# A grouped convolution with a mixture of experts behind it: aggregation on 32 by 64 tiles ahead of the first convolution, weights at the head of both load queues

## What is computed

```
x = x + conv(x, L0_weight, 9 taps, 4 groups) + (cond @ c_weight.T)[:, :, None] + fside[None, :, None]
h   = gelu(gelu(cond @ W0 + b0) @ W1 + b1)
att = softmax(h @ W2 + b2)                       # 128 samples by 8 experts
x = x + einsum('boi,bih->boh', einsum('bk,koi->boi', att, weight), x) + (att @ bias_k)[:, :, None]
```

## Time and profile before

| | us |
|---|---|
| median of 3 runs | 252.88 (252.79 to 253.17) |
| the profiled execution | 252.83 |
| its span in the profile | 251.0 |

### The profile page before, as it was taken

The page is one execution under the profiler, slowest core; times in us unless marked ns, Lnnn a source line. Parts: engine busy times, 40 slices in busy tenths (PEclk is TensorE's granted clock), DMA queues, the critical chain, the costliest instruction groups (busy, mean ns, idle before and its releaser), DMA issues.

```text
span 251.0 us, 5804 instructions
## 1 busy us (share of the span) xinstructions
PE 239.5 (95%) x2180; PEld 95.4 (38%) x2180; DVE 223.1 (89%) x146; ACT 89.5 (36%) x144; POOL 27.1 (11%) x52
## 2 busy tenths in 40 slices
PE   7399999999999999999999999999999999999973
PEld 5263233333333333333333344344444444434531
DVE  0531899999999999999999999999999999999683
ACT  2305353321433333341505233333415052333453
POOL 1030422010101010010101010100101010101000
PEclk9659999999999999999999999999999999999999
DMA  6999693999999999999999999998989998444376
GB/s 145 262 306 274 136 200 60 334 231 407 329 375 240 381 240 339 293 319 305 272 350 238 387 228 373 276 361 249 335 292 287 342 262 347 167 167 168 123 293 256
DMA packets 29770, 68.72 MB, mean 274 GB/s; under 512 B 3312, under 2 KB 5616, under 8 KB 29760
## 3 DMA queue, kind: packets, MB, share of 16 engines
q1 hardware_dynamic: 19824, 51.41, 63.0%
q10 hardware_dynamic: 9936, 17.17, 26.2%
HBM read 35.02 MB, written 33.55 MB: 273 GB/s over the span
## 4 chain that ended last, share of the span: by engine, by line
PE 93%; DMA 2%; DVE 2%; SPq 1%; issue 0%; ACT 0%; DVEq 0%
PE yps L534 64%; PE zps L557 21%; DMA xin<-in_x 2%; PE yps L616 2%; PE yps L573 2%; PE zps L516 2%; DVE xph L414 1%; SPq L199 1%; DVE ynat L483 1%; PE zps L596 0%; PE yps L596 0%; PE zps L585 0%; PE zps L634 0%; DVE ycol L476 0%; ACT xin L380 0%
## 5 line engine op out<-in xcount | busy, mean ns | idle before, releaser
L534 PE MATMUL yps<-xph,wraw 64*64 64x512 f32 x1488 | 167.4, 591 | 0.0
L308 ACT ACTIVATE zout<-zps,gamu 128x512 f32<-128x512 f32 x120 | 72.9, 688 | 130.9 <-PE zps L557 87.9
L534 PEld LDWEIGHTS yps<-xph,wraw 64*64 64x64 f32 x1488 | 60.0, 132 | 100.2 <-issue 99.8
L422 DVE STREAM_TRANSPOSE ycol<-yps 128x1024 f32<-128x1024 f32 x62 | 74.5, 1220 | 9.2 <-PE yps L534 8.5
L414 DVE STREAM_TRANSPOSE xph<-xin 128x2112 f32<-128x2112 f32 x32 | 74.8, 2339 | 2.5 <-DMA xin<-in_x 2.5
L432 DVE STREAM_TRANSPOSE ynat<-ycol 128x2048 f32<-128x2048 f32 x30 | 67.6, 2291 | 1.1
L557 PE MATMUL zps<-ynat,mixv 64*64 64x512 f32 x480 | 57.6, 589 | 0.0
L244 POOL COPY mixv<-mixt 128x512 f32 (+1 forms) x16 | 17.5, 1094 | 178.9 <-ACT zout L308 174.5
L557 PEld LDWEIGHTS zps<-ynat,mixv 64*64 64x64 f32 x480 | 19.9, 132 | 30.3 <-issue 29.3
L316 ACT ACTIVATE mixt<-zps 128x1024 f32<-128x1024 f32 x8 | 7.8, 1021 | 17.3 <-PE zps L516 17.3
L616 PE MATMUL yps<-zout 128*128 128x256 f32 x20 | 8.9, 632 | 2.2 <-POOL zout L250 1.3
(11 more groups left out here) (54 smaller groups left out, 29.1 us busy)
## 6 DMA issues: line engine op xcount, KB each, us to landing
out<-zout SPq DMA_DIRECT2D x60, 512.0 KB, 5.3
xin<-in_x ACTq DMA_DIRECT2D x60, 258.0 KB, 7.5
xin<-in_x SPq DMA_DIRECT2D x60, 258.0 KB, 7.3
out<-xin SPq DMA_DIRECT2D x2, 512.0 KB, 3.2
out<-xin SPq DMA_DIRECT2D x4, 256.0 KB, 2.2
xin<-in_x ACTq DMA_DIRECT2D x4, 132.0 KB, 5.0
xin<-in_x SPq DMA_DIRECT2D x4, 130.0 KB, 5.0
xin<-in_x SPq DMA_DIRECT2D x4, 128.0 KB, 6.7
```

What stands on the lines that cost most here:

```text
L308: nc.scalar.activation(zout[:, o].rearrange("p (i c j q) -> p c i j q", i=2, c=2, q=PH)[:, c], zps[:, at:at + BANK].rearrange("p (q i j) - ...
L422: nc.vector.transpose(ycol[:, :, :, :, :, g].rearrange("p i s j q c -> p (i s j) q c"), yps[:, 2 * BANK * (g % 2):2 * BANK * (g % 2) + 2 * ...
L534: last = nc.tensor.matmul(yps[C * c:C * c + C, at:at + BANK].rearrange("p (s f) -> p s f", s=S // 2), wsum[rows, b, g], xph[slot][c][rows, ...
```

## The change

- The expert weights are stored once (64 columns, 128 KB instead of 256 KB). `aggregate` has two steps instead of four; each step has 8 matmuls on tiles of 32 by 64, four row tiles by two column tiles, where one column tile gives one half of the output channels and the other the other half. `mixt` now holds each matrix once.
- Both steps stand ahead of the first convolution group, with `keep_on(3)` before the attention's matmul, before the first step and before the second; `keep_on(6)` is gone. The output constants come after the first block of group 1, the pair constants after group 3.
- ScalarE instead of VectorE spreads the attention, in four instructions. ScalarE instead of GpSimd fills `mixv`, in four instructions per unit (each 64 partitions by 256 elements, from either half of `mixt` to either half of `mixv`), behind evacuation 1 and the loads of the unit before.
- SyncE's queue starts with `mlps`, `shares`, `mixw`, then all of x of unit 0; ScalarE's starts with `wraw`. ScalarE's loads of unit 1 are issued in two blocks, around the spreading of the attention; its load of unit 2 comes right after the gathers.
- VectorE's first two phase transposes follow each other, and both of unit 1 come one place earlier.

```diff
-        mixt = sb("mixt", [P, C, NS])
+        mixt = sb("mixt", [P, CH // 2, RT * RO, NS])
...
-        mixw = zout[:, 1, 0:CH * P].rearrange("p (a c) -> p a c", a=CH)
-        consts = zout[0:CK, 1, CH * P:]
+        mixw = zout[:, 1, 0:CH * C].rearrange("p (a c) -> p a c", a=CH)
+        consts = zout[0:CK, 1, 2 * CH * C:]
...
+        def mix_places(slot, h, d):
+            return mixv[slot][C * h:C * h + C].rearrange("p b (a d c) -> p d b a c", a=CH // 2, d=2)[:, d]
+        def mix_values(u, d):
+            return mixt[C * d:C * d + C, :, :, bass.ds(S * u, S)].rearrange("p a c b -> p b a c")
...
             sp.dma_start(mlps[:], mlp).then_inc(mlp_in, 16)
-            for k in range(KQ):
-                for t in range(2):
-                    sp.dma_start(*x_piece(0, 0, 0, k, t, 0)).then_inc(x_first, 16)
             sp.dma_start(shares[:], share).then_inc(share_in, 16)
-            for k in range(KQ):
-                for t in range(2):
-                    sp.dma_start(*x_piece(0, 0, 0, k, t, 1)).then_inc(x_in[0], 16)
-            sp.dma_start(wraw[:], conv_w).then_inc(w_in, 16)
+            sp.dma_start(mixw, mix_w).then_inc(mix_in, 16)
+            for part, there in ((0, x_first), (1, x_in[0])):
+                for k in range(KQ):
+                    for t in range(2):
+                        sp.dma_start(*x_piece(0, 0, 0, k, t, part)).then_inc(there, 16)
...
-                nc.gpsimd.tensor_copy(mixv[slot][:], mixt[:, :, bass.ds(S * u, S)].rearrange("p c b -> p b c")
-                                      ).then_inc(mixv_made, 1)
...
+            def matrices(u, slot):
+                for h in range(2):
+                    for d in range(2):
+                        nc.scalar.activation(mix_places(slot, h, d), mix_values(u, d), ACT.Copy).then_inc(mixv_made, 1)
...
+            act.dma_start(wraw[:], conv_w).then_inc(w_in, 16)
             for k in range(KQ):
                 for t in range(2):
                     act.dma_start(*x_piece(0, 0, 1, k, t, 0)).then_inc(x_first, 16)
...
-            act.dma_start(mixw, mix_w).then_inc(mix_in, 16)
...
-            load(1, 1)
+            load_block(1, 1, 0)
+            act.wait_ge(share_in, 16)
+            act.wait_ge(mm, 4)
+            for o in range(RO):
+                nc.scalar.activation(attt[:, o], sps[:, 0:NS], ACT.Copy, scale=turn[:, o:o + 1]).then_inc(soft, 1)
+            load_block(1, 1, 1)
             gather(0, 0)
             gather(0, 1)
             gather(1, 0)
             gather(1, 1)
+            load(2, 0)
...
                         evacuate(2 * i + c - 4, c, o)
                         if o == 1:
                             load(2 * i + c, c)
+                            matrices(2 * i + c - 3, 1 - c)
...
-            dve.wait_ge(mm, 4)
-            nc.vector.tensor_tensor(attt, sps[:, 0:NS].unsqueeze(1).broadcast_to([P, RO, NS]),
-                                    turn.unsqueeze(2).broadcast_to([P, RO, NS]), ALU.mult).then_inc(soft, 1)
             phases(0, 0, 1)
             y_columns(0, 0)
+            phases(1, 1, 0)
             y_columns(0, 1)
-            phases(1, 1, 0)
+            phases(1, 1, 1)
             y_columns(0, 2)
-            phases(1, 1, 1)
             y_columns(0, 3)
...
-                    nc.tensor.matmul(zps[:, BANK * r:BANK * r + BANK], mixw[32 * r:32 * r + 32, a],
-                                     attt[32 * r:32 * r + 32].rearrange("p o b -> p (o b)"),
-                                     start=True, stop=True).then_inc(agg_mm, 1)
+                    for d in range(2):
+                        nc.tensor.matmul(zps[C * d:C * d + C, BANK * r:BANK * r + BANK],
+                                         mixw[32 * r:32 * r + 32, 2 * a + d],
+                                         attt[32 * r:32 * r + 32].rearrange("p o b -> p (o b)"),
+                                         start=True, stop=True).then_inc(agg_mm, 1)
...
+            keep_on(3)
             pe.wait_ge(share_in, 16)
             pe.wait_ge(soft, 3)
             nc.tensor.matmul(sps[:, 0:NS], att[:].rearrange("p o e -> p (o e)"), eye,
                              start=True, stop=True).then_inc(mm, 1)
-            pe.wait_ge(turned, 1)
-            keep_on(6)
+            keep_on(3)
+            first_aggregate()
+            keep_on(3)
+            second_aggregate()
             pe.wait_ge(w_in, 16)
-            conv(0, 0, 0, (first_aggregate,))
-            conv(0, 0, 1, (second_aggregate,))
-            conv(0, 0, 2, (output_constants, None, third_aggregate))
-            conv(0, 0, 3, (None, None, fourth_aggregate))
-            conv(1, 1, 0, (None, None, pair_constants))
+            pe.wait_ge(w_sum, 1)
+            conv(0, 0, 0)
+            conv(0, 0, 1, (output_constants,))
+            conv(0, 0, 2)
+            conv(0, 0, 3, (None, None, pair_constants))
+            conv(1, 1, 0)
             conv(1, 1, 1)
             mix(0, 0, 0)
```

More of the change, by code:

```diff
@@ L237, in _, with constants_of @@
         def _(pool):
-            def matrices(u, slot):
+            def constants_of(u, slot):
                 if not (isinstance(u, int) and u < 2):
                     pool.wait_ge(z_made, 8 * u - 8)
-                if isinstance(u, int) and u == 0:
-                    pool.wait_ge(agg_out, 2 * CH)
-                nc.gpsimd.tensor_copy(mixv[slot][:], mixt[:, :, bass.ds(S * u, S)].rearrange("p c b -> p b c")
-                                      ).then_inc(mixv_made, 1)
                 if isinstance(u, int) and u == 0:
@@ L259, in _ @@
             for a in range(CH):
-                own = mixw[:, a].rearrange("p (d h g c) -> p d h g c", d=2, h=2, g=G)[:, :, :, a]
-                nc.gpsimd.tensor_tensor(own, own, same.rearrange("p (h c) -> p h c", h=2).unsqueeze(1)
-                                        .broadcast_to([P, 2, 2, 8]), ALU.add).then_inc(mix_eye, 1)
+                own = mixw[:, a].rearrange("p (h g c) -> p h g c", h=2, g=G)[:, :, a]
+                nc.gpsimd.tensor_tensor(own, own, same.rearrange("p (h c) -> p h c", h=2), ALU.add).then_inc(mix_eye, 1)
             pool.wait_ge(w_in, 16)
@@ L282, in _, with load_block @@
                                         ALU.mult, ALU.mult).then_inc(const_sum, 1)
-            matrices(0, 0)
-            matrices(1, 1)
+            constants_of(0, 0)
+            constants_of(1, 1)
             with pool.Fori(1, NU // 2) as i:
                 for c in range(2):
-                    matrices(2 * i + c, c)
+                    constants_of(2 * i + c, c)
         @block.scalar
         def _(act):
+            def load_block(u, slot, k):
+                for t in range(2):
+                    act.dma_start(*x_piece(slot, u, 1, k, t)).then_inc(x_in[slot], 16)
             def load(u, slot):
-                if not (isinstance(u, int) and u < 2):
-                    act.wait_ge(turned, 2 * u - 2)
+                act.wait_ge(turned, 2 * u - 2)
                 for k in range(KQ):
-                    for t in range(2):
-                        act.dma_start(*x_piece(slot, u, 1, k, t)).then_inc(x_in[slot], 16)
+                    load_block(u, slot, k)
             def evacuate(u, slot, o):
@@ L343, in _ @@
             gather(1, 1)
+            load(2, 0)
             act.wait_ge(const_mm, 1)
             nc.scalar.activation(gprod.rearrange("p e c -> p (e c)"), gps, ACT.Copy).then_inc(const_out, 1)
-            load(2, 0)
-            gather(2, 0)
-            gather(2, 1)
-            gather(3, 0)
-            gather(3, 1)
+            act.wait_ge(agg_out, CH)
+            matrices(0, 0)
             act.wait_ge(gam_mm, 1)
@@ L356, in _ @@
                     load(3 + o // 2, 1 - o // 2)
+                if o == 1:
+                    matrices(1, 1)
             for o in range(PR):
@@ L360, in _ @@
                     load(5, 1)
+                    matrices(2, 0)
             with act.Fori(3, NU // 2) as i:
@@ L369, in _ @@
                     evacuate(u, u % 2, o)
+                    if o == 1:
+                        matrices(u + 1, 1 - u % 2)
             act.wait_ge(gam_cut, NU)
@@ L619, in first_aggregate @@
             def first_aggregate():
-                pe.wait_ge(soft, 4)
+                pe.wait_ge(soft, 7)
                 pe.wait_ge(beta_made, 2)
-                pe.wait_ge(mix_eye, 1)
-                pe.wait_ge(w_sum, 1)
+                pe.wait_ge(mix_eye, 2)
                 aggregate(0)
             def second_aggregate():
-                pe.wait_ge(mix_eye, 2)
+                pe.wait_ge(mix_eye, 4)
                 aggregate(1)
@@ L695, in _ @@
             mix(NU - 2, 0, 3)
-            pe.wait_ge(mixv_made, NU)
+            pe.wait_ge(mixv_made, 4 * NU)
             pe.wait_ge(last_nat, 2)
@@ L763 @@
     residual, parity, pairs, turn, same = constants()
-    mix_w = a["L1_cond_weight"].reshape(KE, CH, RT, RO, C).transpose(2, 3, 0, 1, 4).reshape(P, CH, C)[:, :, K_CH]
```

(1 more changed line is left out.)

18 lines of the change are left out of this document (5 added, 13 removed).

## The result

The changed kernel takes 251.75 us, the median of 17 runs, against 252.88 for the kernel before: a ratio of 0.9955 with a 95% interval of 0.994 to 0.997. It is faster by 1.1 us, under half a per cent, but clear of the noise; 4.2 were forecast, and 251.75 lies above the range (247.2 to 251.3). The profiled execution took 251.26, with a span of 249.5 us (before: 252.83 and 251.0). One of the 17 executions took 421.1 us at a mean granted clock of 0.56 and does not count in the ratio.

A forecast was written before the change was run, and what follows sets the result against it. VectorE and TensorE both bound the steady state, VectorE slower by a hair. Along VectorE, -1.46 (start), -2.42 (unit 0), 0 (steady units) and -0.3 (tail) sum to -4.2, from 252.83 to 248.7 us; range 247.2 to 251.3.

The forecast's parts named there:

- Bounds: Steady units: both TensorE (13.76 us a unit) and VectorE (13.78) bound, VectorE slower by a hair.
- Part 1: Prelude: first convolution starts at 17.6 us, VectorE's first column transpose at 20.3 against 21.76; -1.46 us.
- The hole: Loads from 3.3 to 4.8 us moved just 55 GB/s; weights at the head may fill this, worth up to 1.5 us.
- Part 2: Unit 0 on VectorE, first column transpose to that of unit 1: from 17.32 to 14.9 us; -2.42 us.
- Part 3: Steady units: VectorE unchanged, ScalarE's four copies at 0.48 us each (1.9) fit in 2.9 us of room; 0 us.
- 0.7 that TensorE can be late at group 3: Steady units: TensorE's allowed lateness before VectorE waits, 0.7 us of the 2.9 us of room for ScalarE's copies.
- the slower rival: Steady units: ScalarE's copies above 2.9 us together delay mix 1, group 3, then VectorE; 263 us at 1.0 each; chance 0.07.
- Part 4: Tail: TensorE stands about 0.3 us behind VectorE instead of 0.6, so the tail ends earlier; -0.3 us.
- Late x: Unit 0 or 1: x late because 884 KB stand ahead; 249.5 to 250.5 us; chance 0.15.
- The slow prelude: TensorE's prelude: clock stays at 0.50 or eight tiles run as two sets; 250.5 to 252.3 us; chance 0.12.

The follow-up runs named there:

- profile with short fillers: Changed kernel with copies before the load issue and last unit's copies moved earlier, each keep_on(3) cut to keep_on(1): 251.89 us, ratio 0.9865; profiled run 252.01.
- both edits: Changed kernel with ScalarE's copies before the load issue and the last unit's copies behind evacuation 3 of unit 13: 249.64 us (0.9857), again 248.94 (0.9864).
- one more filler: Changed kernel with copies before the load issue, last unit's copies moved earlier, plus keep_on(1) behind the small network's second-layer matmul: 248.58 us, ratio 0.9849.
- the two kernels with 2.46 and 2.71 us: 2.46: kernel before with ScalarE instead of GpSimd filling `mixv`, four copies per unit, 254.17 us, ratio 1.0043; 2.71: the changed kernel, 251.75 us.

## Why the prediction was wrong

- **Bounds.** Right: VectorE had no slack in the steady state, its unit is 13.784, and it was 13.78 again in every kernel with the copies well placed, halved or left out, but for the profile with short fillers. The view that showed it was VectorE's waits, not the shares.
- **Part 1, the start.** Right in size: -1.58 for -1.46, the convolution at 17.3 for 17.6, but partly by luck, for the split was not as told. With the granted clock at 1.00 in the profile, TensorE's chain was through at 16.2, 1.4 us before my 17.6, and x at 14.67 was last. In other runs TensorE was slow in the prelude, as in the first profile with both edits, where the aggregation ended at 18.6 and VectorE's first column transpose came at 21.44 (timeline; the change took 1.56 us for these six records):

```profile
8.61 2.93 PE L635 MATMUL yps<-zout 128*128 128x256 f32 x6
```

The windows of that profile give a granted clock of 1.00 all the same. Six such records took 2.93 us also in the profile with one more filler, where the windows give 0.50 from 9 to 11 us. So I take the clock as low here too, and the window's figure as no proof against it. The hole was filled, as hoped; x still landed no earlier than 14.1, in the upper half of my 13.1 to 15.0. The median lies 0.5 above the profiled execution (251.75, 251.26), which I had not allowed for; this spread of the prelude may be why, but no other execution of the change was profiled. The rule on semaphore tails of the Trainium skill ("TensorE: Matmul & The Clock Gate", section "The cost: per-tile semaphore tail") would add 0.12 us per step, an estimate by that page. The trace shows less where it can be read: the first gather came 1.23 us after the step's start here and 1.20 before, in the same view, 0.03 us more. It waits for the first half of the increments only, four here and two before; for the second half no row tells.
- **Part 2, unit 0.** Right: -2.47 for -2.42, with VectorE's two short waits (0.15 and 0.52 us) where told. x of unit 1 came in time.
- **Part 3 is the step that failed**: "The price of a copy is not shown: [...] I take 0.48 [...] It fits, at the upper end too (2.4)." A copy of half of the elements on half of the partitions took 0.66 us, more than the upper bound, and the starts are 0.68 apart: four take 2.71. The room was too large as well: I counted 2.9 us, and the two kernels with 2.46 and 2.71 us put it at about 2.5. It took both errors: 2.71 us would have fitted into 2.9, and 1.9 into 2.5. The "0.7 that TensorE can be late at group 3" was the room's softest part: TensorE trails VectorE by 0.67 us from unit 2 on (49.51 against 48.84; before, 0.89 at unit 2 and 0.67 at unit 15). In unit 1 its group 3 waited 0.22 us for columns 1, at 39.82; for the later units no wait is noted. The mechanism had been written down as the slower rival, with this place and these neighbours; its price per copy was taken from instructions that read PSUM, while these read SBUF, at a step of 512 bytes. The step alone does not explain the price, for the evacuations read PSUM at the same step; nor does the crossing of the partition halves, for the copies that stay in their half took 0.66 us too. What makes them dear is open. The loss fell between the forecast's 0 and the rival's: 0.92 us in 14 units.
- **Part 4 failed too**: the tail was costed with TensorE's position alone, -0.3. The copies of the last unit, which the diff places in exactly this stretch, were not followed there. They cost 0.6 us of TensorE's waiting and 0.85 in the last transfers; 0.17 is the lag from the steady units. And the -0.3 itself does not exist: without copies the tail is 18.94 us, as before. TensorE's lag at the start of a unit settles at 0.66 to 0.74 us in both kernels, from 0.95 in unit 1 before and 0.66 in unit 2 without copies, so it does not carry the start of the run into the tail.
- **Rivals.** Late x (0.15) did not come. The slow prelude (0.12) is real in single runs at a third of its price. The slower case was the right place with too high a threshold.
- **Two slips of arithmetic**, which do not move the forecast. In the slower rival 0.3 x 13 is 3.9, not 4.2; and a copy of 256 elements between 0.37 at 128 and 0.61 at 512 comes to 0.45, not 0.48.

## What to carry to other kernels

An instruction added to an engine that is busy a third of the time is not free: look in its order at what stands behind it, and whether it sits before or after the engine's own long wait. Here one line, ahead of the wait for the phases or behind it, is worth 0.9 us in the loop. A margin has two sides, the work put in and the room for it; here either error alone would have done no harm. A copy placed for the steady state must be followed into the tail by itself. And where a change moves compute ahead of a transfer, the transfer's order has to move with it.

## What the runs showed of the hardware

- Four ScalarE copies of 64x256 elements, SBUF to SBUF, started 0.57 us apart when both kept the same half of the partitions and 0.67 to 0.69 when source or target changed half; a single one took 0.62 to 0.69, 0.66 on the mean, in every case. An evacuation of 128x512 from PSUM takes 0.69: half the partitions and half the elements, from SBUF, saved nearly nothing.
- With pieces of x at the head of both queues behind `mlps` (packets of 0.9 KB on the mean), the DMA engines moved 101 to 123 GB/s from 3 to 5 us at a busy share of 0.6 to 0.8; with `shares`, `mixw` and `wraw` ahead of x (1.5 KB on the mean), 356 to 388. With 544 KB more of weights in front of it, x of unit 0 was complete at 14.1 to 15.0 us, against 14.07 before and 15.85 with `wraw` behind it in the changed queues.
- Eight matmuls on 32 by 64 tiles ran as fast as four on 32 by 128: 1.12 us and 1.14 in the timeline for 512 columns each.
- The same prelude ran at either clock from run to run. With three fillers of three matmuls TensorE was back at full pace by 12 to 14.3 us, and VectorE's first column transpose came at 19.6 to 21.4; with three of one it stayed at 1.2 GHz to beyond 18 us in the profiled run, and four of six runs took 3 to 4.4 us longer than the other two.
- The granted clock of a window may not be a full record: it read 1.00 in a profile whose fillers took 2.93 us for six records, as long as with 0.50 in another and against 1.56 at full pace.
